# Transposing the next tile's rows behind the features instead of behind the logits, in the graph stage of a two-layer kernel

## The reference

```python
self_feat = concat(v, q if the row's sum is not 0 else 0) @ W_self.T + b_self
output = self_feat
for d in range(2):
    aff = einsum('bnhd,bmhd->bnhm', qh, kh) / sqrt(32)      # 16 heads, 20 columns m
    w   = softmax(where(cond > 0, aff, NEG) + label_bias)
    output += einsum('bnhf,hgf->bnhg', einsum('bnhm,bmf->bnhf', w, kv), Wout[d]) + bout[d]
x = v + relu(output)
```

## Time and profile before

| | us |
|---|---|
| median of 3 runs | 3061.3 |
| lowest and highest | 3059.5, 3061.43 |
| profiled execution, its own time | 3061.68 |
| profiled execution, its span | 3059.8 |
| graph stage in the trace, first logits to last values | 137.4 to 453.1 |
| tables of the graph layer | up to 137 |

### The profile page before, as it was taken

The page is one execution under the profiler, slowest core; times in us unless marked ns, Lnnn a source line. Parts: engine busy times, 40 slices in busy tenths (PEclk is TensorE's granted clock), DMA queues, the critical chain, the costliest instruction groups (busy, mean ns, idle before and its releaser), DMA issues.

```text
span 3059.8 us, 61633 instructions
## 1 busy us (share of the span) xinstructions
PE 3018.5 (99%) x24578; PEld 2403.3 (79%) x24578; DVE 1827.1 (60%) x2694; ACT 1366.4 (45%) x2840; POOL 804.2 (26%) x523
## 2 busy tenths in 40 slices
PE   8999999999999899999999999999999999999998
PEld 5899988888888677777777777777788888878887
DVE  4489972211222788888888888888566433433332
ACT  2266652222221677777777777777222211111111
POOL 1011112000000344444444444446454101111110
PEclk9999999999999999999999999999999999999999
DMA  5643314333333343333333333332673000010100
GB/s 180 230 177 115 115 65 151 106 106 108 105 104 117 107 110 84 85 94 88 91 102 88 84 86 90 91 95 81 208 263 127 28 20 16 28 35 28 35 14 14
DMA packets 198177, 296.28 MB, mean 97 GB/s; under 512 B 28008, under 2 KB 105992, under 8 KB 196136
## 3 DMA queue, kind: packets, MB, share of 16 engines
q1 hardware_dynamic: 189060, 286.34, 30.0%
q0 software_dynamic: 576, 6.29, 0.6%
q10 hardware_dynamic: 8292, 0.05, 0.2%
HBM read 189.13 MB, written 102.18 MB: 95 GB/s over the span
## 4 chain that ended last, share of the span: by engine, by line
PE 64%; DMA 1%; DVE 1%; ACT 0%; issue 0%; POOL 0%; SPq 0%; DVEq 0%; POOLq 0%; ACTq 0%
PE b_po L1499 16%; PE b_ps L1470 12%; PE d_pf L1973 12%; PE d_po L1984 11%; PE b_tp_act L1482 7%; PE c_po L1746 4%; PE b_tp_dve L1482 3%; DMA c_ot<-o_t 1%; PE d_pt L1965 0%; DVE c_ol L1762 0%; DVE o_first_rest L1762 0%; ACT b_p L1438 0%; ACT c_oh L1707 0%; POOL d_y L1914 0%; DVE norm_st L983 0%
## 5 line engine op out<-in xcount | busy, mean ns | idle before, releaser
L1529 DVE TENSOR_REDUCE b_nm<-b_ps 128x1 f32<-128x1024 f32 x512 | 602.1, 1217 | 17.6 <-PE b_ps L1470 4.5
L1438 ACT ACTIVATE b_p<-b_ps,b_nm 128x1024 f32<-128x1024 f32 x512 | 564.6, 1112 | 29.2 <-DVE b_nm L1529 29.2
L1499 PE MATMUL b_po<-b_pt,b_v 128*64 128x256 f32 x4096 | 498.3, 385 | 0.8 <-DVE b_pt L1549 0.8
L1443 ACT ACTIVATE b_pt<-b_tp_act 128x512 f32<-128x512 f32 x512 | 307.9, 601 | 305.4 <-PE b_tp_dve L1482 305.4
L1549 DVE COPY b_pt<-b_tp_dve 128x512 f32<-128x512 f32 x512 | 351.5, 687 | 117.0 <-PE b_tp_dve L1482 116.9
L1482 PEld LDWEIGHTS b_tp_act<-ident,b_p 64*128 64x128 f32 x4096 | 311.5, 138 | 118.2 <-issue 100.6
L1499 PEld LDWEIGHTS b_po<-b_pt,b_v 128*64 128x64 f32 x4096 | 272.0, 136 | 128.5 <-ACT b_pt L1443 0.9
L1482 PE MATMUL b_tp_act<-ident,b_p 64*128 64x64 f32 x4096 | 347.6, 225 | 2.4 <-issue 2.4
L1482 PE MATMUL b_tp_dve<-ident,b_p 64*128 64x64 f32 x4096 | 348.0, 225 | 0.0
L1948 ACT ACTIVATE d_ge<-d_pf,b_t 128x512 f32<-128x512 f32 x128 | 88.2, 689 | 579.9 <-PE d_pf L1973 579.9
L1482 PEld LDWEIGHTS b_tp_dve<-ident,b_p 64*128 64x128 f32 x4096 | 311.8, 138 | 14.7
(11 more groups left out here) (302 smaller groups left out, 6115.9 us busy)
## 6 DMA issues: line engine op xcount, KB each, us to landing
b_raw_q<-q_t SPq DMA_DIRECT2D x124, 256.0 KB, 4.2
q_t<-p_qk SPq DMA_DIRECT2D x64, 256.0 KB, 2.0
k_t<-p_qk SPq DMA_DIRECT2D x64, 256.0 KB, 2.0
v_n<-p_vs SPq DMA_DIRECT2D x32, 512.0 KB, 3.2
b_v<-v_n SPq DMA_DIRECT2D x32, 512.0 KB, 3.9
b_raw_k<-k_t SPq DMA_DIRECT2D x124, 128.0 KB, 4.3
c_ot<-o_t SPq DMA_DIRECT2D x7, 2048.0 KB, 10.1
a_x<-x SPq DMA_DIRECT2D x32, 256.0 KB, 3.2
```

Of the source, the lines that this page charges most:

```text
L1438: act.activation(pr[k % 4][:], ps[k % 2][:], ACT.Exp, bias=nm[:, k % 4:k % 4 + 1], accum_out=rs[:, n:n + 1]).then_inc(exp_done, 1)
L1443: act.activation(dst, src, ACT.Copy).then_inc(t_out[0], 1)
L1499: mm = pe.matmul(po[rows, (blk % 2) * 2 * P:(blk % 2 + 1) * 2 * P], vt[u][:, kc, rows], pt[blk % 2][h][:, kc, :], start=(kc == 0), stop=(k ...
L1529: dve.tensor_reduce(nm[:, k % 4:k % 4 + 1], ps[k % 2][:], axis=AX.X, op=ALU.max, negate=True).then_inc(max_done, 1)
```

## The change

In TensorE's loop the call `transposes(k + 1)` moves from directly behind `logits(k)` to directly behind `features(k)`. It now stands directly ahead of `values(k - 1)`. Nothing is added or removed, and the lists of the other engines are the same as before.

```diff
                 logits(k)
-                if k + 1 < n:
-                    transposes(k + 1)
                 if k:
                     weights(k - 1)
                 features(k)
+                if k + 1 < n:
+                    transposes(k + 1)
                 if k:
                     values(k - 1)
```

## The result

The changed kernel takes 3154.17 us (median of 4 runs, 3145.71 to 3157.69) against 3060.73 us before. The ratio is 1.0301 with a 95% interval of 1.0288 to 1.0314: 93.4 us slower, where 58.7 were forecast. The direction was right, and the size was not.

What follows compares the result with a forecast made beforehand. TensorE, busy for 99% of the span, was taken to set the pace. 57.3 us for thirty tiles plus 1.4 us for the first, added to 3061.3 us, gave 3120 us, with a range of 3110 to 3131.

Steps and rivals of the forecast that it cites:

- The cover that goes: Values wait for ScalarE's weight copies, held behind its casts: 1.91 us per tile, 57.3 us over 30 tiles.
- The first tile: In iteration 0 the logits directly behind the transposes wait for a_xl: 1.4 us more than before.
- What was priced at nothing for VectorE: VectorE's later sum and bias in each tile: ready just in time, lateness absorbed by a 2.3 us pause, no cost.
- Idle time and the clock: TensorE's new pauses of 1.8 us per tile leave the granted clock at 1.00, at no cost.
- The rival on the clock: Each of 30 pauses brings a low-clock stretch of 2.64 us: 79 us more, 3199 us; chance 0.05.
- Features that get cheaper: Features speed up without ScalarE's PSUM reads beside them: priced at 2 us, 3118 us; not slower overall, chance 0.02.

Runs made afterwards that it cites:

- e3: The changed kernel with ten more 320-column matmuls in each of the 30 pauses ahead of the values: 3116.36 us, ratio 1.0176.
- e4: The changed kernel with thirteen 128-column transposes in each of the 30 pauses ahead of the values: 3113.08 us, ratio 1.0168.
- e5: The changed kernel with five more 320-column matmuls in each of the 30 pauses ahead of the values: 3112.32 us, ratio 1.0167.
- e1: The changed kernel with ScalarE's three copies of the weights put ahead of its two casts of the next tile: 3076.66 us, ratio 1.0047.
- e2: The changed kernel with the transposes directly ahead of the features, behind the weights, instead of behind the features: 3061.02 us, ratio 1.0003.
- e6: The changed kernel with the transposes inside the features, behind 10 of their 13 matmuls: 3102.12 us, ratio 1.0131.
- e9: The kernel before the change with 46 identity transposes in the wait ahead of the stage's first logits: 3059.39 us, ratio 0.999.

## Why the prediction was right in direction and wrong in size

**The cover that goes: right.** The chain from the last row transpose to the values was forecast at 1.92 us and measured at 1.90, so the delay of the values was 1.79 instead of 1.81. The profile shows the wait as 1.63 us of idle time, since it counts from the modelled end of the last transpose. With full clock a tile takes 11.54 us (in e3, L787 starts from 145.6 to 491.7), 1.88 above before; the forecast had 1.91. Where the clock stayed up in the stage, the whole loss was 55.3 us (e3), 52.0 (e4) and 50.0 (e5), against 58.7. Thirty tiles at 1.88 and the first tile give 57.8, so the price per tile holds; the totals are a few us lower, within what these kernels differ by from run to run. e1 shows that it hangs on ScalarE's order, e2 that it vanishes with a cover of 3.1 us, and e6 that a cover of 0.7 us takes part of it.

**The first tile: right.** The logits wait 1.6 us for a_xl there, once.

**What was priced at nothing for VectorE: right.** It has its pause (2.1 us on average, 2.3 forecast), and there is no wait of TensorE for VectorE apart from the first tile and the end of the stage.

**Idle time and the clock: wrong.** The step that failed is "A pause of 1.8 us lies between the two and is nearer to the first, so I price it at nothing". The forecast put the clock at nothing, and behind 20 of the 30 pauses of 1.63 us it fell, which cost about 37 us (3154 us with idle pauses, 3116 with matmuls in them). The row it rested on, a clock of 1.00 around a pause of 0.99 us at the end of the stage, was also only one draw. In e2 the end of the stage is the same and has nearly the same pauses (0.64 and 0.99 us, against 0.61 and 0.99), and there the clock does fall. Its timeline and stretches:

```profile
446.98 0.87 PE L835 MATMUL a_pw<-ident,a_lg 128*120 128x128 f32 x6 [0.64 <-DVE a_lg L952]
448.84 3.01 PE L843 MATMUL a_po<-a_bd,a_wt 120*128 120x96 f32 x12 [0.99 <-ACT a_wt L717]
```

```profile
448.00:450.00 2.00, 1.16 (x5) 1.16 (x6) 0.00 (x0) 0.79 (x3) 0.32 (x1) 0.62 0.35 131
450.00:452.00 2.00, 2.00 (x10) 1.76 (x9) 0.00 (x0) 0.11 (x1) 0.00 (x0) 0.50 0.03 8
```

The twelve matmuls of the values take 3.01 us here and 1.69 in the earlier trace rows, with the same instructions directly ahead of them. In e9, whose order in this stage is that of the kernel before, the clock falls there too (448 to 456 us). One execution that shows full clock behind a pause does not show that the pause is free.

**The rival on the clock: the right mechanism, with too small a chance and too high a price.** It got 0.05 and 79 us, from 2.64 us per pause, taken from the stretch behind 5.8 us of idle time. A low stretch costs 1.57 us here, or 3.06 for the long kind, and follows two pauses in three. The rival did say that the time lies in between if only some pauses bring one. The range should have reached to it: by the rival's price five such pauses leave 3131 us. The Trainium skill, "TensorE: Matmul & The Clock Gate", HAM oscillation, names this mechanism for long gaps; the pauses here are shorter than its rule asks for, and the clock fell all the same.

**Features that get cheaper: not seen.** In the changed kernel's timeline four of the 512-column matmuls take 1.07 to 1.17 us, as before, and nothing was given back.

What stays open is why a given pause is or is not followed by a low stretch. The traces, one for each kernel, show 0 of 30 at 0.90 us, 20 of 30 and 7 of 15 at 1.63, and 29 of 29 at 2.87. The changed kernel's own time spreads over 12 us from run to run (its fastest run, 3145.71 us, has a mean clock of 0.985, the others 0.983), while before spreads over 2 to 9. Which pauses are hit within one execution was not explained.

## What to carry to other kernels

When a step moves in one engine's list, look in the other engines' lists for what stands behind the instruction that waits for it: the copies that were held back here had nothing to do with the moved transposes, except that they stood behind their casts. Measure the cover, not the distance: with 3.1 us of work between the transposes and the values the move was free, with 0.7 us it cost 40 us, with none 93.

Where a change like this one opens a pause on TensorE in each round of a loop, add the clock to the wait, and do not take one quiet row of the old trace for its price; harmless matmuls or transposes in the pause give the clock back and show how large its part is.

## What the runs showed of the hardware that was not expected

Idle time of TensorE well below 2 us brought the granted clock down to the level of 1.2 GHz: of 30 pauses of 1.63 us, in a stage where TensorE is busy 87% of the time, 20 were followed by a low stretch, which cost about 34 us in 397. Thirty pauses of 0.90 us, in the same place and behind five matmuls more, were not (e5). Two pauses of about 0.6 and 0.99 us close to each other at the end of the stage were followed by a low stretch in some traces (e2, e9, the changed kernel) and not in others (before, e5). Transposes kept the clock at 1.00 where idle time did not (e4), and 46 of them in a wait for a transfer made the 26 matmuls behind it run at full clock (e9).
